# A four-network graph kernel: a shorter lead of the one-hot compares, more unread products in the chain, the edge tables' turns moved, row products moved into rounds

## What is computed

```python
x = x + _L0_gnn_ref(h, ...)   # graph convolution
x = x + _L1_gnn_ref(h, ...)   # convolution, then attention of two heads of 128
x = x + _L2_gnn_ref(h, ...)   # five gated steps of width 256, then a two-layer MLP
x = x + _L3_gnn_ref(h, ...)   # attention of eight heads of 8, then of one head of 128
```

```python
logits = leaky_relu(a_src[src] + a_dst[dst], NEG_SLOPE)
m = segment_max(logits, dst)
e = exp(logits - m[dst])
out = segment_sum(h[src] * (e / segment_sum(e, dst)[dst]), dst)
```

## Time and profile before

| | us |
|---|---|
| median of three runs | 3230.16 (3226.15 to 3234.99) |
| the profiled execution | 3232.75 |
| its span, first to last instruction | 3231.0 |
| TensorE busy | 2855.9 (88%) |
| VectorE busy | 1864.3 (58%) |
| ScalarE busy | 1374.1 (43%) |
| GpSimd busy | 927.2 (29%) |
| mean granted TensorE clock | 0.93 |

### The profile page before, as it was taken

The page is one execution under the profiler, slowest core; times in us unless marked ns, Lnnn a source line. Parts: engine busy times, 40 slices in busy tenths (PEclk is TensorE's granted clock), DMA queues, the critical chain, the costliest instruction groups (busy, mean ns, idle before and its releaser), DMA issues. The chain is left out here.

```text
span 3231.0 us, 46643 instructions
## 1 busy us (share of the span) xinstructions
PE 2855.9 (88%) x15991; PEld 2223.9 (69%) x15991; DVE 1864.3 (58%) x4907; ACT 1374.1 (43%) x2657; POOL 927.2 (29%) x713
## 2 busy tenths in 40 slices
PE   5777888999996999999999999999966866777997
PEld 3445785677775878778787787887445766665775
...
DMA packets 92994, 266.57 MB, mean 83 GB/s; under 512 B 22080, under 2 KB 73111, under 8 KB 83063
## 3 DMA queue, kind: packets, MB, share of 16 engines
...
## 5 line engine op out<-in xcount | busy, mean ns | idle before, releaser
L3357 PE MATMUL psum<-gate_stream,parts 128*128 128x384 f32 (+1 forms) x3600 | 669.4, 344 | 7.5 <-ACT x L3397 4.4
L3357 PEld LDWEIGHTS psum<-gate_stream,parts 128*128 128x128 f32 x3600 | 631.5, 189 | 24.6 <-ACT x L3397 6.0
L3462 POOL CAST gate_stream<-gate_adj 128x1920 fp32r<-128x1920 f16 (+1 forms) x200 | 371.4, 1865 | 839.3 <-PE psum L3357 827.8
L2698 PE MATMUL psum<-gat_h,gat_pair 128*128 128x129 f32 (+1 forms) x3750 | 539.5, 289 | 20.3 <-DVE gat_pair L2506 18.3
L2698 PEld LDWEIGHTS psum<-gat_h,gat_pair 128*128 128x128 f32 (+1 forms) x3750 | 455.0, 190 | 132.3 <-DVE gat_pair L2506 69.1
L3496 DVE SCALAR_TENSOR_TENSOR gate_work<-psum,bhh,gate_work 128x384 f32<-128x384 f32 (+1 forms) x80 | 50.1, 626 | 777.5 <-PE psum L3304 761.8
L1823 POOL DMA_INDIRECT edge_rows<-edge_table,src_idx x366 | 394.4, 1078 | 173.4 <-issue 111.3
L2506 DVE SCALAR_TENSOR_TENSOR gat_pair<-gat_above,gat_adj 128x512 f32<-128x512 f32 (+3 forms) x475 | 304.4, 641 | 72.2 <-ACT gat_above L2609 35.5
L2600 ACT ACTIVATE psum<-gat_ad_rows,gat_as 128x512 f32<-128x512 f32 (+3 forms) x525 | 334.9, 638 | 18.0 <-PE psum L2730 1.2
L2609 ACT ACTIVATE gat_above<-psum,gat_as 128x512 f32<-128x512 f32 (+3 forms) x525 | 324.5, 618 | 38.4 <-PE psum L2686 35.9
L2459 DVE SCALAR_TENSOR_TENSOR gat_acc<-gat_adj,gat_q,gat_acc 128x512 f32<-128x512 f16 (+3 forms) x449 | 308.7, 697 | 0.0
...
## 6 DMA issues: line engine op xcount, KB each, us to landing
...
```

Source lines behind the costliest of these rows:

```text
L2698: mm = e.matmul(ps[0:p, b, a:a + D + 1], pair[:, g % 2, i * P:i * P + p], h1[:, hi, h, :], start=hi == 0 and i % 3 == 0, stop=hi == NT - 1 ...
L3357: mm = e.matmul(ps[:, f, 0:hi - lo], parts[:, t, m, f, :], stream[:, (NGG * i + t // GG) % GR, 0:windows(i), t % GG * W:(t % GG + 1) * W], ...
L3462: e.tensor_copy(stream[:, n % GR, 0:windows(i), :], cols[:, i % 2, 0:windows(i), g * GW:(g + 1) * GW]).then_inc(widened, 1)
```

## The change

It has four parts.

1. VectorE's compares may run at most LEAD = 8 ahead of the products, not 24 (the ring keeps its 24 buffers). The last chunk draws 8 steps, not 10, and gathers 48, not 46.
2. In each chunk's chain the 14 unread products become 8 behind `line_up`, 12 behind `carries_of` and 24 ahead of the sums.
3. The edge tables' turns: two tables in step last - 1 of the MLP's loop, two in step last, the rest behind `turn(last)`. The loop's drain is written out, with 22 unread products in it and another order on ScalarE.
4. In both dense layers the rows stages of spans 1 to 6 leave the place in front of round 0. Each is put at the start of one of the first rounds (12 rounds with two heads, 6 with one), its copy on ScalarE behind that round's `exp`. Unread products ahead of `rows(0)` are 8, not 4, and there are none in a round that has a stage.

```diff
-DRAWN = (4, 12, 12, 12, 12, 12, 10)
+DRAWN = (4, 12, 12, 12, 12, 12, 8)
-WARM = 14
+LEAD = 8
+WARM = (8, 12, 24)
...
-                    if n >= RING:
-                        e.wait_ge(pulled, n - RING + 1)
+                    if n >= LEAD:
+                        e.wait_ge(pulled, n - LEAD + 1)
...
                     line_up(c)
+                    self.keep_busy(e, ps[:, 6, :], WARM[0])
...
                     carries_of(c)
+                    self.keep_busy(e, ps[:, 7, :], WARM[1])
...
-                    self.keep_busy(e, ps[:, 6, :], WARM)
+                    self.keep_busy(e, ps[:, 6, :], WARM[2])
                     sums(c)
...
-        stages = ([("rows", 0, h) for h in range(heads)] + [("own", n, 0) for n in range(ng)] +
-                  [("rows", u, h) for h in range(heads) for u in range(1, nu)])
-        after_turn = 2
+        stages = [("rows", 0, h) for h in range(heads)] + [("own", n, 0) for n in range(ng)]
+        early = len(stages)
+        stages += [("rows", u, h) for u in range(1, nu) for h in range(heads)]
+        bank_of = lambda m: m % 4 if m < early else 2 + m % 2
+        in_round = lambda g: early + g - 1 if 1 <= g <= len(stages) - early else None
...
                     exp(g)
+                    if in_round(g):
+                        take(in_round(g))
...
-                for m in range(len(stages) - after_turn):
+                for m in range(early):
                     stage(m)
                 for h in range(heads):
                     turn(0, h)
-                for m in range(len(stages) - after_turn, len(stages)):
-                    stage(m)
...
-                e.wait_ge(copied, len(stages))
-                self.keep_busy(e, ps[:, 3, :], 4)
+                e.wait_ge(copied, early)
+                self.keep_busy(e, ps[:, 3, :], 8)
                 rows(0)
...
                 for g in range(every):
+                    if in_round(g):
+                        stage(in_round(g))
...
-                    if 0 < g <= lead:
+                    if not in_round(g) and 0 < g <= lead:
...
-                    if q == last + 2:
+                    if q == last - 1:
                         e.wait_ge(folded, 1)
-                        e.wait_ge(added, last + 1)
-                        edges.tensor_turn(e)
+                        edges.tensor_places(e)
+                    if q == last:
+                        edges.tensor_valid(e)
...
+                ease(last)
+                ease_last(last - 1)
+                edges.scalar_last(e)
+                keep(last - 4)
+                root(last - 2)
+                ease_last(last)
+                norm(last - 3)
+                root(last - 1)
+                keep(last - 3)
+                norm(last - 2)
+                root(last)
+                keep(last - 2)
+                norm(last - 1)
+                norm(last)
+                keep(last - 1)
+                keep(last)
```

140 lines of the change are left out of this document (90 added, 50 removed).

## The result

| us | before | changed | change |
|---|---|---|---|
| median | 3232.57 (four runs) | 3214.45 (3210.41 to 3215.82, four runs) | -18, ratio 0.9942 [0.9928, 0.9956] |
| profiled execution, its span | 3232.75, 3231.0 | 3215.82, 3214.0 | -16.9 |
| the same in a later set | 3233.65 (eleven runs) | 3216.16 (seven runs) | -17, ratio 0.9947 [0.9927, 0.9967] |

What follows compares the result with a forecast made beforehand. GpSimd's gathers were taken to set five periods of the eight-head stage. Terms -26.2 - 1.7 - 9 - 6.5 + 1 + 5 = -37.4 took the profiled 3232.75 us to 3195.4, on the median's scale 3193; range 3177 to 3214.

Steps and rivals of the forecast that it cites:

- Gathers and lead: Eight-head stage, chunks 1 to 6: a lead of 8 ends the long gathers, chain 1 to 6 falls to 334.9 us, gain 26.2.
- rival 4: Eight-head chunks: a lead of 8 is too short and TensorE waits; break-even 10.6 us per chunk, possibly 3262 us; 4%.
- The clock: Eight-head chunks 1 to 5: more unread products raise TensorE's clock for the sums, about 3 us each, hidden under the gathers.
- Chunk 0: Eight-head stage, first chunk: a higher clock when the sums start, gain 1.7 us, half of 3.4 since compares start late.
- Last chunk: Eight-head chunk 6, no gather following: high clock when the sums start, gain 9 us, bounds 0 and 9.75.
- rival 2: Eight-head sums: the clock is not high when they start, so gains of 9 and 1.7 us fall away, 3204 us; 10%.
- Drain: End of the stage before the eight heads: edge tables' transposes moved among full pieces, gain 6.5 us, bounds 3 and 9.
- Two heads: Two-head dense layer: moved row products idle TensorE at the start and slow the rounds, loss 5 us (gain 1, loss 20).
- Single head: Single-head dense layer: start 7.7 us earlier, six rounds lose 8.5 at the half clock, loss 1 us (gain 7, loss 4).
- Rivals 1: Eight-head gathers: GpSimd's time beside the compares is only spread, not saved; the 26.2 us falls away, 3221 us; 12%.
- 5: Eight-head chunks: the stalls come from something else in phase with a chunk's start; shares the spread-not-saved rival's time and 12%.
- rival 3: Both dense layers: moved row products cost nothing and the single head gains its 7 us, 3180 us; 8%.

Runs made afterwards that it cites:

- experiment 2: Kernel before, lead kept at 24, a small VectorE reduction added behind every fourth one-hot compare: 1.0067 on a slow chip, 0.9930 where before takes 3227 us.
- experiment 3: On the kernel before: 8, 12, 24 unread products alone, 1.0042 (slow chip); new drain plus, in the last chunk, these and one behind every sums step, 0.9930.
- experiments 1: Kernel before with only the lead cut from 24: to 8, 1.0103 and 1.0107 (slow chips) and 0.9926; to 16, 0.9954.

## Why the prediction was wrong

The sum said -37.4 and its terms, as measured, give -20. The last chunk makes 6.3 us of the difference, the two heads 4.0, the gathers 3.3, chunk 0 3.1, the single head 0.9; the drain was 0.3 better.

**Gathers and lead (forecast -26.2, got -22.9).** The mechanism was right: experiment 2 shows it. What failed is the step "TensorE and VectorE without the waits need 328.1, less the clock below and less 25 x 0.18 = 4.5", 308.6 in rival 4, and what follows there, "so they stay behind GpSimd". They needed 328.1, and GpSimd waited for them in every period, 7.1 us between chain 1 and chain 6, for which the sum had nothing. GpSimd's own part was shorter than forecast (338.2 - 7.1 = 331.1 for 334.9), and that hid half of the miss.

The missing 19.5 are two terms. The lead's price, which rival 4 named and gave 4%, is real at 1.6 us per chunk (7.9 / 5), far from its 10.6. The clock, for which I had 3 us in each of five chunks, gave next to nothing: the sums of chunks 1 to 4 took 198.0 us, and 199.0 in the kernel with only the lead, and the five chains 92.7 and 94.5, so 3 us in all instead of 15. In two of the five chunks the clock at the start was higher than before by 0.29, in the others hardly or not. The products no longer drawn gave their 4.5 (chunk 5's sums 36.2 for 41.0 with the lead alone, 4.8 with what the clock did there).

**Chunk 0 (-1.7, got +1.4).** The products alone gained nothing there, and the lead alone cost 2. The sum had no term for the lead in this chunk. Chunk 0 varies, though: 64.4 to 66.7 in nine profiles with a lead of 24, 65.8 to 67.9 in nine with 8.

**Last chunk (-9, got -2.7).** "With 44 products in a 19 us chain I expect the high level when the sums start": it was high, and fell at 2883, so the step that failed is that a high clock at the start carries through the sums; the price of that was in the bounds (0, if the clock is lost again) and not in the term. I had read the earlier trace rows as a clock that was low because of the chain. This is rival 2's effect with another cause, and experiment 3 shows that cause: in the changed kernel, its repeat and the kernel without rounds the clock was high when the sums began and fell within 3 us, and with the unread product behind each step it stayed. It was in the rows: the last sums ran 19.5 us at 0.50 while TensorE was busy throughout.

**Drain (-6.5, got -7.6, by all profiles -6.8).** Right.

**Two heads (+5; by all profiles +9.0).** "Twelve rounds at 4.1 for two lose 1.4" compared all twelve with a cadence of 1.93 that holds for the first eight or nine; the last four were at 1.39 and 0.86, and lose 4.3 together. The start lost 0.7 (I had 1), the low clock 2.6 in all by one profile (I had about as much). So the mechanism held and the term was mis-sized, by what the rounds replace.

**Single head (+1; by all profiles +1.9).** Start 7.9 for 7.7, rounds 10.0 for 8.5: a pair takes up to 7.8, not 6.7, because a row product takes 2.0 us and a `total_of` 1.16 at the half clock, not 1.75 and 0.86. The mechanism was right.

Rivals 1 (spread, not saved) and 5 are excluded by experiments 1 and 2, rival 3 by the single head's rows. With the sizes that the runs gave, the sum would have been +9.0 + 1.9 - 6.8 + 1.4 - 22.9 - 2.7 = -20, and the measured change is -18.
